# Edge sum of a graph network on one core: steps of 64 nodes in place of 128, and a list of 824 steps in place of 728

## What is computed

```python
# layer 0
agg = segment_sum(x[src], dst);  mean = agg / max(degree, 1)
h = relu(concat([x, mean]) @ W_fc + b_fc) + x @ W_res + b_res
x = layernorm(x + h)
# layer 1, twice (relu between), then layernorm(x + out)
msg = x[src] @ Wm + bm + edge_attr @ We + be
out = segment_sum(msg, dst) + x @ Ws + bs
```

## Time and profile before

| | |
|---|---|
| median of 3 runs | 5270.2 us |
| the runs | 5269.23, 5270.2 and 5283.6 us |
| the profiled execution, its own time | 5251.91 us |
| its span, first to last instruction | 5250.1 us |
| mean granted TensorE clock over the span | 0.875 |
| busy shares: TensorE, its weight loads, VectorE, ScalarE, POOL | 72%, 61%, 47%, 30%, 43% |

### The profile page before, as it was taken

The page is one execution under the profiler, slowest core; times in us unless marked ns, Lnnn a source line. Parts: engine busy times, 40 slices in busy tenths (PEclk is TensorE's granted clock), DMA queues, the critical chain, the costliest instruction groups (busy, mean ns, idle before and its releaser), DMA issues.

```text
span 5250.1 us, 120588 instructions
## 1 busy us (share of the span) xinstructions
PE 3801.8 (72%) x39993; PEld 3184.3 (61%) x39993; DVE 2493.0 (47%) x6331; ACT 1577.5 (30%) x2106; POOL 2248.7 (43%) x2698
## 2 busy tenths in 40 slices
PE   0257677778877777577777688877887687787774
PEld 0245566665555555466667677766776576676763
DVE  6377666766655656477776422222222222222224
ACT  0133355555555555477775200000002000000000
POOL 6321233334333434222222555555555655555552
PEclk9589989988898998899999888888888888888886
DMA  2702234344444444466664677776775777676774
GB/s 94 79 34 84 111 138 164 141 161 167 164 166 165 165 165 165 135 189 188 188 187 112 198 248 259 253 243 237 268 249 171 248 248 246 232 248 238 250 244 133
DMA packets 331871, 968.01 MB, mean 184 GB/s; under 512 B 151102, under 2 KB 244417, under 8 KB 274402
## 3 DMA queue, kind: packets, MB, share of 16 engines
q1 hardware_dynamic: 272086, 873.36, 47.5%
q0 software_dynamic: 59712, 93.77, 7.5%
HBM read 706.74 MB, written 263.39 MB: 185 GB/s over the span
## 4 chain that ended last, share of the span: by engine, by line
PE 54%; issue 19%; DVE 10%; another core or an unknown queue 4%; ACT 4%; DVEq 3%; POOL 3%; DMA 2%; ACTq 0%; SPq 0%; POOLq 0%
PE ps L1014 38%; PE ps L1035 9%; PE ps L1006 4%; DVE union L729 3%; DVE union L832 2%; ACT union L1315 2%; PE ps L1079 2%; ACT abuf L1297 2%; DVE abuf L843 1%; DVEq L409 1%; POOL msg L1166 1%; DVEq L843 1%; POOL union L1120 1%; DMA msg<-y_tab,idx 0%
## 5 line engine op out<-in xcount | busy, mean ns | idle before, releaser
L1166 POOL DMA_INDIRECT msg<-y_tab,idx x1776 | 1829.5, 1030 | 2135.4 <-ACT idx L1277 1615.5
L1014 PE MATMUL ps<-union,abuf 128*128 128x192 bf16 x14504 | 1567.0, 268 | 359.2 <-issue 318.8
L1014 PEld LDWEIGHTS ps<-union,abuf 128*128 128x128 f16 x14504 | 1345.9, 107 | 545.6 <-issue 489.0
L729 DVE TENSOR_TENSOR union<-lane,union 128x512 f16<-128x512 f16 (+3 forms) x2048 | 985.3, 531 | 492.0 <-PE ps L1035 265.8
L1297 ACT ACTIVATE abuf<-ps 128x784 f16<-128x784 f32 x1184 | 923.6, 822 | 884.0 <-PE ps L1035 596.5
L1035 PE MATMUL ps<-union 128*128 128x196 f16 (+2 forms) x4096 | 712.8, 309 | 411.1 <-ACT abuf L1297 169.7
L1014 PE MATMUL ps<-early,abuf 128*128 128x195 bf16 x7350 | 806.7, 264 | 0.0
L1014 PEld LDWEIGHTS ps<-early,abuf 128*128 128x128 f16 x7350 | 708.2, 106 | 69.8 <-issue 18.3
L1035 PEld LDWEIGHTS ps<-union 128*128 128x128 f16 x4096 | 337.3, 111 | 641.1 <-ACT abuf L1297 366.1
L1277 ACT ACTIVATE idx<-src_g 128x8 int32 (+1 forms) x222 | 46.0, 208 | 2117.1 <-PE ps L1006 1891.8
L1079 PE MATMUL ps<-union 128*64 128x128 f32 x7280 | 479.2, 278 | 173.3 <-ACT union L1315 157.8
(11 more groups left out here) (229 smaller groups left out, 1192.2 us busy)
## 6 DMA issues: line engine op xcount, KB each, us to landing
abuf<-a_dram SPq DMA_DIRECT2D x296, 1568.0 KB
a_dram<-abuf SPq DMA_DIRECT2D x74, 3136.0 KB
union<-in_edge_attr_dram SPq DMA_DIRECT2D x728, 160.0 KB, 2.4
msg<-y_tab,idx POOLq DMA_INDIRECT x1776
y_tab<-union SPq DMA_DIRECT2D x28, 336.0 KB, 2.9
y_tab<-early SPq DMA_DIRECT2D x7, 682.5 KB, 9.8
abuf<-x_pad SPq DMA_DIRECT2D x7, 448.0 KB
abuf<-x_pad SPq DMA_DIRECT2D x14, 224.0 KB, 2.9
```

The costliest lines, as they stand in the source:

```text
L729: return V.tensor_tensor(to.rearrange("p s (c u) -> p s c u", u=2), lanes.unsqueeze(1).to_broadcast([P, HB, width // 2, 2]), codes[:, whic ...
L1014: last = nc.tensor.matmul(ps[:, bank, 0:3 * width_of[r]], abuf[:, buffer, hi * P:(hi + 1) * P], ycols[r][:, hi, :], start=hi == 0, stop=hi ...
L1166: pool.indirect_dma_start(msg[:, s, 0:3 * width_of[r]], None, y_tab[r], bass.IndirectOffsetOnAxis(ap=idx[:, s:s + 1], axis=0)).then_inc(ga ...
```

## The change

A step now covers half a block: 64 nodes. There are 196 such parts in place of 98 blocks, so the path has more steps, and marking, widening, multiplication and addition handle 64 columns in place of 128. The group of 640 edges, the eight buffers, the lag of four and the turn of eight steps stay. The sums lie in the same tile, seen as 196 pieces of 64 columns. Since part numbers go to 195, the helper that unpacks four numbers from a word masks eight bits of each.

```diff
+    EW = P // 2
+    PARTS = BLOCKS * P // EW
-    ESTEPS = -(-(GROUPS + BLOCKS - 1) // EB) * EB
+    ESTEPS = -(-(GROUPS + PARTS - 1) // EB) * EB
...
-        def load_blocks(frm, n):
+        def load_blocks(frm, n, top=BLOCKS - 1):
...
-                    for v in packed for b in (v & 0x7F, (v >> 8) & 0x7F, (v >> 16) & 0x7F, v >> 24)]
+                    for v in packed for b in (v & 0xFF, (v >> 8) & 0xFF, (v >> 16) & 0xFF, (v >> 24) & 0xFF)]
...
+            step(V.tensor_single_scalar(blast_i, ends, EW.bit_length() - 1, op=ALU.arith_shift_right))
+            step(V.tensor_copy(blast, blast_i))
...
-            step(V.tensor_scalar(e_blk, e_blk, float(BLOCKS - 1), None, ALU.min))
+            step(V.tensor_scalar(e_blk, e_blk, float(PARTS - 1), None, ALU.min))
...
-            step(V.scalar_tensor_tensor(e_base, e_blk, float(P), e_base, ALU.mult, ALU.add))
+            step(V.scalar_tensor_tensor(e_base, e_blk, float(EW), e_base, ALU.mult, ALU.add))
...
                         marks = V.tensor_tensor(mark_e[:, h, :, :].rearrange("p j (c u) -> p j c u", u=2),
-                                                lane16[:, 0:P].rearrange("p (c u) -> p c u", u=2).unsqueeze(1)
-                                                .to_broadcast([P, EG, P // 2, 2]),
-                                                rel_e[:, h, :, :].unsqueeze(2).to_broadcast([P, EG, P // 2, 2]),
+                                                lane16[:, 0:EW].rearrange("p (c u) -> p c u", u=2).unsqueeze(1)
+                                                .to_broadcast([P, EG, EW // 2, 2]),
+                                                rel_e[:, h, :, :].unsqueeze(2).to_broadcast([P, EG, EW // 2, 2]),
...
-                        to = flat(sums_e[:, bass.ds(bs[h], 1), :])
-                        V.tensor_tensor(to, to, ps[:, b, 0:P], ALU.add).then_inc(e_add, 1)
+                        to = flat(sums_w[:, bass.ds(bs[h], 1), :])
+                        V.tensor_tensor(to, to, ps[:, b, 0:EW], ALU.add).then_inc(e_add, 1)
...
-                                last = nc.tensor.matmul(ps[half:half + D, h, 0:P], feats[:, h, j * D:(j + 1) * D],
+                                last = nc.tensor.matmul(ps[half:half + D, h, 0:EW], feats[:, h, j * D:(j + 1) * D],
                                                         hot_e[:, h, j, :], start=j < 2, stop=j >= EG - 2)
```

More of the change, by code:

```diff
@@ L247, in gnn_program @@
         feats = union[:, 0:EB * EG * D].rearrange("p (s c) -> p s c", s=EB)
-        mark_e = union[:, EB * EG * D:EB * EG * (D + P // 2)].bitcast(F16).rearrange("p (s j c) -> p s j c", s=EB, c=P)
-        hot_e = union[:, EB * EG * (D + P // 2):EB * EG * (D + P // 2 + P)].rearrange("p (s j c) -> p s j c", s=EB, c=P)
+        mark_e = union[:, EB * EG * D:EB * EG * (D + EW // 2)].bitcast(F16).rearrange("p (s j c) -> p s j c", s=EB, c=EW)
+        hot_e = union[:, EB * EG * (D + EW // 2):EB * EG * (D + EW // 2 + EW)].rearrange("p (s j c) -> p s j c", s=EB, c=EW)
         sums_e = af[:, :].rearrange("p (b c) -> p b c", c=P)
-        assert EB * EG * (D + P // 2 + P) <= UNION and EG * GROUPS + TW <= YW0 and HIS == BLOCKS
+        sums_w = af[:, :].rearrange("p (b c) -> p b c", c=EW)
+        assert EB * EG * (D + EW // 2 + EW) <= UNION and EG * GROUPS + TW <= YW0 and HIS == BLOCKS
         FB = 512 // D
@@ L410, in load_blocks @@
                 words[0:1, bass.ds(frm, n // 4)], engines=(ENG.DVE,), min_val=0,
-                max_val=(BLOCKS - 1) * 0x01010101,
+                max_val=0x7FFFFFFF,
                 skip_runtime_bounds_check_because="four block numbers, each clamped when the path was made")
-            return [nc.s_assert_within(b, 0, BLOCKS - 1, skip_runtime_bounds_check_because="one of the four block numbers")
-                    for v in packed for b in (v & 0x7F, (v >> 8) & 0x7F, (v >> 16) & 0x7F, v >> 24)]
+            return [nc.s_assert_within(b, 0, top, skip_runtime_bounds_check_because="one of the four block numbers")
+                    for v in packed for b in (v & 0xFF, (v >> 8) & 0xFF, (v >> 16) & 0xFF, (v >> 24) & 0xFF)]
         def flat(v):
@@ L823, in _ @@
                     dve.sem_inc(free, 1)
-                step(V.memset(ps[:, EB - LAG:EB, 0:P], 0.0), "zeros_e")
+                step(V.memset(ps[:, EB - LAG:EB, 0:EW], 0.0), "zeros_e")
                 with dve.Fori(0, ESTEPS // EB) as i:
-                    bs = load_blocks(i * (EB // 4) + (SPAD + G - LAG) // 4, EB)
+                    bs = load_blocks(i * (EB // 4) + (SPAD + G - LAG) // 4, EB, PARTS - 1)
                     for h in range(EB):
@@ L841, in _ @@
                         dve.wait_ge(e_add, i * EB + (h + EB))
-                        to = flat(sums_e[:, bass.ds(bs[h], 1), :])
-                        V.tensor_tensor(to, to, ps[:, b, 0:P], ALU.add).then_inc(e_add, 1)
-                last = load_blocks((SPAD + ESTEPS + G - LAG) // 4, LAG)
+                        to = flat(sums_w[:, bass.ds(bs[h], 1), :])
+                        V.tensor_tensor(to, to, ps[:, b, 0:EW], ALU.add).then_inc(e_add, 1)
+                last = load_blocks((SPAD + ESTEPS + G - LAG) // 4, LAG, PARTS - 1)
                 for k in range(LAG):
@@ L847, in _ @@
                     dve.wait_ge(e_add, ESTEPS + k + EB)
-                    to = flat(sums_e[:, bass.ds(last[k], 1), :])
-                    V.tensor_tensor(to, to, ps[:, EB - LAG + k, 0:P], ALU.add).then_inc(e_add, 1)
+                    to = flat(sums_w[:, bass.ds(last[k], 1), :])
+                    V.tensor_tensor(to, to, ps[:, EB - LAG + k, 0:EW], ALU.add).then_inc(e_add, 1)
                 dve.wait_ge(e_add, ESTEPS + LAG + EB)
```

## The result

The change took 5407.5 us (median of 4, 5373.5 to 5421.0) where the kernel before took 5276.9 on the same chip (median of 4, 5269.2 to 5287.4): ratio **1.0236, interval 1.0183 to 1.0290**, 131 us slower. The forecast was 5329, the range 5306 to 5360. The sign was right; the loss is more than twice the forecast 59 us. The profiled execution took 5401.2 us for 5251.9.

A forecast was written before the change was run, and what follows sets the result against it. No engine was full; a chain or SP's uncounted queue set the pace, SP becoming the bound. Terms 61.5 - 3.2 + 1, about +59 us, on the median 5270.2 gave 5329 us, range 5306 to 5360.

The forecast's parts named there:

- SP becomes the bound: Edge sum: SP's turn stays 6.78 us over 103 turns, adding 61.5 us; the end behind the last issue saves 3.2.
- TensorE waiting for landing rows: Edge sum, a sign of being right: TensorE idle for a landing of edge rows, more than 1.5 us once per turn.
- Behind the last issue: End of the edge sum: 3.8 us from last issue to last addition's end, against 7.0 before, so -3.2 us.
- Widths: Edge-sum steps at 64 columns: marking 0.32 us, widening 0.69, addition 222 ns, all leaving the chain below SP's 6.78 us.
- Rival A: Edge sum: SP's turn falls, the shorter chain sets 5.3 to 5.9 us, kernel faster at 5178 to 5239 us; chance 0.05.
- Rival B: Edge sum: TensorE's clock falls and TensorE becomes the bound; half way, 7.6 us per turn adds 84 us; chance 0.04.
- Register work elsewhere: Gather additions of all rounds: extra mask instructions, 67 us if nothing hid them, taken as 0 with 22 as upper end.
- The range: Whole kernel: 5306 to 5360 us, from leftover SP waits, register work, missing additions and the spread of executions.

The follow-up runs named there:

- e3: The changed kernel with SP taking each step's group from its loop counter instead of the register load, so summing other groups; ratio to the kernel before 0.9974.
- e5: The changed kernel unaltered, run again on another chip with a second profile; ratio to the kernel before 1.0254.
- e7: The changed kernel with old masks in the gather additions and two of SP's eight loads per turn issued by ScalarE; ratio to the kernel before 1.0137.
- e6: The kernel before, unaltered, profiled again; it took 5278 us in its group, rounds 1 and 2 at 1074 and 1078 us.
- e18: The kernel before with VectorE's marking of the next pass moved ahead of the eighth gather addition in rounds 1 and 2; ratio 1.0092.
- e8: The kernel before with a second mask on each block number, 12 more register instructions per pass on VectorE; ratio 1.0284.
- e14: The kernel of e8 (second mask on each block number, on the kernel before) run again in a later group; ratio to the kernel before 1.0409.
- e15: The kernel before with twelve masks per pass on ScalarE's queue in rounds 1 and 2, as e9, run again; ratio 1.0000.
- e16: The kernel before with VectorE loading eight unpacked block numbers per pass in rounds 1 and 2, run again; ratio 1.0016.
- e12: The kernel before with one more 128x512 memset per pass on VectorE in rounds 1 and 2; ratio 1.0009.
- e13: The changed kernel unaltered, run a third time, in a later group; ratio to the kernel before 1.0126.
- e1: The kernel before with only the helper's eight-bit masks from the change, steps staying 728 of 128 columns; ratio 1.0047.
- e4: The kernel before with one small preparation product done twice, so TensorE's later code lies where the changed kernel's does; ratio 0.9992.
- e9: The kernel before with twelve masks per pass put on ScalarE's queue in rounds 1 and 2; ratio 0.9986.

## Why the prediction was right, and where it failed

- **SP becomes the bound, +61.5 less 3.2: right.** First to last issue 701.4 us for 702.7, the turn 6.78 for 6.78, the eight-number load never under 1.649 us in 103 turns, TensorE waiting for landing rows (1.46 us per turn, a little under the 1.5 named). Behind the last issue 4.0 us remain, for a forecast 3.8. The edge sum is 58 to 60 us longer in every pair, and e3 removes SP's load and with it 110 us.
- **Widths: nearly right.** Markings 320 ns as read off the line, additions 221 for 222, widenings 737 for 690. They hung on nothing. By their groups VectorE's marks and additions are 444 us for a forecast 445, ScalarE's widenings 302 for 284, so the line drawn through two larger sizes was 7% low there.
- **Rival A** (a shorter chain sets the pace) was right about the chain (5.58 us a turn in e3, for 5.3 to 5.9) and wrong about who leads; SP's turn stayed 6.78. In e3, where SP's load is gone, the stretch is 585 us and the kernel as fast as before.
- **Rival B: half right, and a term is missing.** The clock fell (0.74) and TensorE stayed under 6.78 us per turn, as weighed. But the sum has no term for what comes behind: the 98 folding products at the end of the edge sum took 39.8 us for 22.1 in the change's profile, at a granted clock of 0.53. In e5 they took 22.1 at the full clock. The term is worth 0 to 18 us.
- **Register work elsewhere, "I take 0, with 22 us as the upper end": this step failed.** It cost 59 us in the profiled pair and 70 in the second one, both rounds together. The count and the duration were right: four instructions in each pass. That the masks cause it is shown: without them the rounds are back (e7 against e5 and e6). The cover was wrong, and so was the question. I had asked who waits for the additions, and nobody was seen to. The marking behind them on the same queue slides by 0.2 us in the median, in many passes past the moment at which it held up the fourth gather. Those went from 61 of 123 to 24 of 124, at some 2 us each; a part came back where the marking then held up the fifth (over 1.6 us long in 19 passes for 5). This way from the masks to the time is read from the traces and borne out by e18 in so far as moving the marking alone changes the time; it is not shown beyond that. For twelve instructions the price was some 70 us a round (e8 against e6) and 95 (e14 against e15 and e16); where the stalls were absent, the half microsecond of e12 on the same queue cost nothing.
- **The range** ended some 14 us under the fastest run. In e13, where the same change cost 69 us (1.0126), the range would have held in proportion, but by luck: the edge sum is 58.7 us longer there than in e15, rounds 1 and 2 some 42 us longer than in e15 and e16, and round 0 some 29 us shorter. It had no case in which something in the rounds moves, although show TensorE's clock falling there and the earlier trace rows a granted clock of 0.85.

Not settled: why TensorE stalls inside its dense products at all while gathers are being issued; why holding up a gather relieves it; and whether a marking started 4.7 us after the first product in every pass would be faster. By the tables of before (mean 14.65 us, the held-up passes 13.11) that is an estimated 1.5 us in each of 148 passes; no run here does that. No version here beat the kernel before beyond doubt: e3 sums other rows.

## What to carry to other kernels

Before narrowing work, look for the queue whose work per step does not narrow: a register load of 1.66 us and eight issues of 0.583 decided here, and more steps made it worse. An instruction added under an idle engine is not free by that alone: ask what stands behind it on its queue, and with which other engine's work that will coincide. And where a stage has idle time that nothing in the profile explains, leave room in the range for it.

## What the runs showed of the hardware

- One kernel took 5262 to 5401 us in five groups of runs and 4235 in a sixth. It is not the chip alone: e1 to e4 (5398 us) and e9 to e12 (4235) ran on the same chip, some 35 minutes apart. The difference lies in TensorE's idle time by "issue" and the clock that goes with it: in the dense products of round 1, 147 us idle and 269 ns per product before, none and 252 ns in e9.
- GpSimd's gather issue takes 0.95 us alone and up to 2.0 us where it starts while VectorE's marking of 1.23 us runs, while the marking takes at most 1.30 us.
- An f32 product of 64 columns was no shorter at the lower clock than one of 128 at the full one: 281 ns per record in the change's edge sum at a clock of 0.74, 278 in the kernel before (group L1079 of e6's page).
